# Expert down projection: the 32 leftover middle columns of two steps run together, and GpSimd's order of gathers and scatters changes

## The chip, the cores and the metric

One NeuronCore of a Trainium2 chip runs the whole program in one launch. The metric is the device time of a launch in microseconds. Before the change it is 1369.75 us, the median of three runs (1368.03 to 1370.95).

## What is computed

Six layers are applied in turn to 1024 tokens of 512 values in float32: a small feed-forward layer with a memory, an attention layer, the feed-forward layer again, a mixture of experts, a causal attention layer, and the mixture of experts again with the same weights. The change lies in the mixture of experts, which runs twice:

```python
# x: (1024, 512); 8 experts, the best 2 for each token; F = 800 middle columns
logits = xt @ gate_w.T
top_vals, top_idx = top_k(softmax(logits), 2)       # then normalised to sum 1
h1 = einsum('th,efh->tef', xt, w1)                  # up projections
h3 = einsum('th,efh->tef', xt, w3)
act = silu(h1) * h3                                 # 800 middle columns
expert_out = einsum('tef,ehf->teh', act, w2)        # down projection to 512
y = einsum('te,teh->th', w_full, expert_out)
```

## The kernel before

The 2048 pairs of token and expert are sorted by expert into blocks of 32 rows. Four streams (`NSTR` = 4) of 18 blocks each run side by side, so that an execution of this layer is 18 steps (`NSTEP`), and a step works on four blocks, each with its own expert. Stream j owns rows and columns 32j to 32j+31: TensorE is divided into four column quarters, and stream j's results go to PSUM partitions 32j to 32j+31.

A step p has these parts:

- GpSimd gathers 128 rows of tokens from DRAM into `XB` (L880, two buffers). VectorE turns them by blocks of 32 by 32 (L1119).
- `up(p)` on TensorE (L954): 4 chunks of 128 contraction rows, 2 halves of 400 columns, 2 matrices, 4 streams. Each float32 matmul is two instructions in the trace, so that this is 128 instructions. They use all 128 rows of the array and one column quarter each. It needs the step's weights in two halves (`w13_in[0]`, `w13_in[1]`).
- ScalarE applies silu (L1001), VectorE multiplies (L1125) and turns the 800 columns into `ACT_T` (the first 768, L1141) and `ACT_R` (the last 32, L1138).
- `down(p)` on TensorE: the main part (L972) runs over 6 chunks of 128 middle columns, 48 instructions. Then comes the tail (L975) for the last 32 middle columns: for each stream one matmul with 32 contraction rows, 8 instructions. Stream j's activations and weights (`W2B`) lie in partitions 32j to 32j+31, so that its tail uses row quarter j and column quarter j of the array. Main part and tail add into the same PSUM bank, 4 + p % 2. The tail's last instruction raises `m_y`.
- ScalarE copies the bank to `YB` (L1007, two buffers) and GpSimd scatters it to DRAM (L892).

TensorE's order is up(0), up(1), down(0), up(2), down(1) and so on to up(17), down(16), down(17). Between the last two downs there is no up.

SyncE issues the weight loads, in an order written out by hand. Of a step it does: four value loads from the table of experts (L842), the first half of the up weights of the four streams once TensorE is past the first half of the up before (`m_wf`, L848), the second half once that up is done (`m_h`, L850). Then it waits for `m_y` of the down before (L857) and issues, for each stream, the main down weights (L803; stream 3 in two pieces) and the 32 tail rows (L810), nine DMAs. All are conditional: one whose stream keeps its expert is issued, and moves nothing. Main and tail loads count on one semaphore, `w2_in`, and `down(p)` waits for all nine (L965). A first load is made on a guess of the expert before the routing is known (L829 to L833).

GpSimd's order (L885 to L893) is gather 0, gather 1, and then for each p gather p+2 and scatter p. Scatter p waits for ScalarE's copy of step p (`m_yc`).

Other waits on `m_y`: ScalarE's copy (L1007), and VectorE before it overwrites `ACT_T` and `ACT_R` (L1135).

Of the kernel before, what the change touches and what calls it, by code (L numbers as in the profile page):

```python
# [14 lines left out]
P = 128  # L15
# [33 lines left out]
def macaron_program(nc, A, out, stages=6):  # L49

    ctx = ExitStack()
    with ctx:
# [159 lines left out]
        XBT = take([2, C, P])  # L212
        AC = take([FF])
        ACT_T = take([2, FC, P])
        ACT_R = take([2, SR])
        YB = take([2, D])
        W2B = take([D])
        W2_LAST = take([FC // 2, D])
        W13, W2A = [None] * NSTR, [None] * NSTR
        for j in (2, 0, 1):  # L220
# [565 lines left out]
        yl_in = [sem(f"yl_in{i}") for i in range(NT)]  # L786
        LOADS = NSTEP + 1
        N13 = 16 * NSTR
        N2 = 16 * (2 * NSTR + 1)
        assert NSTEP % 2 == 0  # L790

        def up_in(eng, j, a, e, cond=None):

# [11 lines left out]
                              cond=cond).then_inc(w2_in, 16)  # L805
                at += n

        def tail_in(eng, j, e, cond=None):

            eng.dma_start(W2B[SR * j:SR * j + SR], A["w2b"][e].rearrange("e p d -> p (e d)"),  # L810
                          cond=cond).then_inc(w2_in, 16)

        def guess(j):

            return slice(2 * j, 2 * j + 1)
# [7 lines left out]
        def sp_moe(eng, k, f):  # L823
# [2 lines left out]
                eng.wait_ge(s_h, NT * k + i + 1)  # L826
                eng.dma_start(HD[i * P:(i + 1) * P, :], h[:, i, :]).then_inc(S("s_hd"), 16)
            eng.wait_ge(stage_end, 4 * k)
            for j in range(NSTR):  # L829
                tail_in(eng, j, guess(j))  # L830
            eng.wait_ge(S("s_hd"), 16 * NT * (f + 1))
            eng.wait_ge(S("s_lgt"), 4 * f + 4)
            guess_in(eng, f, last)  # L833
# [3 lines left out]
            for p in range(NSTEP + 1):  # L837
                if p < NSTEP:
                    now = []
                    for j in range(NSTR):  # L840
                        q = j * NSTEP + p
                        x = eng.value_load(EBX[q:q + 1, 0:1], min_val=0, max_val=2 * NE - 1)  # L842
                        now.append((bass.ds(x % NE, 1), x >= NE))
                    for a in range(2):
                        if p == 0:
                            eng.wait_ge(w13_in[a], N13 * (LOADS * f + 1))
                        elif a == 0:
                            eng.wait_ge(S("m_wf"), NSTEP * f + p)  # L848
                        else:
                            eng.wait_ge(S("m_h"), 2 * (NSTEP * f + p))  # L850
                        for j in range(NSTR):
                            up_in(eng, j, a, *now[j])
                if p >= 1:
                    if p == 1:
                        eng.wait_ge(w2_in, N2 * (LOADS * f + 1))
                    else:
                        eng.wait_ge(S("m_y"), NSTEP * f + p - 1)  # L857
                    for j in range(NSTR):
                        down_in(eng, j, *late[j])
                        tail_in(eng, j, *late[j])  # L860
                late = now
            if f == 0:
                sp_attn1_weights(eng)
# [9 lines left out]
        def pool_moe(eng, link, k, f):  # L873
# [11 lines left out]
            gather(0)  # L885
            gather(1)
            eng.wait_ge(S("s_sidx"), f + 1)
            for p in range(NSTEP):
                if p + 2 < NSTEP:
                    gather(p + 2)  # L890
                eng.wait_ge(S("m_yc"), NSTEP * f + p + 1)
                eng.indirect_dma_start(YS[:, :], bass.IndirectOffsetOnAxis(ap=SIDX[:, p:p + 1], axis=0),  # L892
                                       YB[:, p % 2, :], None).then_inc(y_out[p % 2], 16)  # L893
            if f == 0:
                pool_front(eng, link, k + 1)

        def pe_moe(eng, k, f):
# [65 lines left out]
            def down(p):  # L963
                G, u = NSTEP * f + p, p % 2
                eng.wait_ge(w2_in, N2 * (LOADS * f + p + 2))  # L965
                eng.wait_ge(S("m_at"), G + 1)
                if G >= 2:
                    eng.wait_ge(S("m_yc"), G - 1)
                for c in range(FC):
                    for j in range(NSTR):  # L970
                        part = W2A[j][c // W2A[j][0].shape[1]]
                        eng.matmul(PS[SR * j:SR * j + SR, 4 + u, :], ACT_T[:, u, c, SR * j:SR * j + SR],  # L972
                                   part[:, c % part.shape[1], :], start=(c == 0), stop=False, skip_group_check=True)
                for j in range(NSTR):
                    mm = eng.matmul(PS[SR * j:SR * j + SR, 4 + u, :], ACT_R[SR * j:SR * j + SR, u, :],  # L975
                                    W2B[SR * j:SR * j + SR, :], start=False, stop=True, skip_group_check=True)
                mm.then_inc(S("m_y"), 1)

            for p in range(NSTEP):
                up(p)  # L980
# [7 lines left out]
        def act_moe(eng, link, k, f):  # L988
# [5 lines left out]
            for p in range(NSTEP + 1):  # L994
                G = NSTEP * f + p
                if p < NSTEP:
                    for hf in range(2):
# [1 line left out]
                        if G > 0:  # L999
                            eng.wait_ge(S("m_at"), G)  # L1000
                        eng.activation(AC[:, hf * FH:(hf + 1) * FH], PS[:, 2 * hf, 0:FH], ACT.Silu).then_inc(S("m_sg"), 1)  # L1001
                if p >= 1:
                    u = (p - 1) % 2
                    eng.wait_ge(S("m_y"), G)
                    if p >= 3 or f == 1:
                        eng.wait_ge(y_out[u], 16 * (NSTEP // 2 * f + (p - 1) // 2))
                    eng.copy(YB[:, u, :], PS[:, 4 + u, :]).then_inc(S("m_yc"), 1)  # L1007
            for u in range(2):
                eng.wait_ge(y_out[u], 8 * NSTEP * (f + 1))
# [6 lines left out]
        def dve_moe(eng, link, k, f):  # L1016
# [110 lines left out]
            for p in range(NSTEP):  # L1127
# [4 lines left out]
                product(G, 1)  # L1132
                eng.wait_ge(S("m_act"), 2 * G + 2)
                if G >= 2:
                    eng.wait_ge(S("m_y"), G - 1)  # L1135
                for a in range(NSTR):
                    rows = slice(SR * a, SR * a + SR)
                    eng.transpose(ACT_R[rows, u, :], AC[rows, FC * P:FF])  # L1138
                    for b in range(NSTR):
                        src = AC[rows, 0:FC * P].rearrange("p (c f) -> p c f", c=FC)  # L1140
                        tr = eng.transpose(ACT_T[SR * b:SR * b + SR, u, :, rows], src[:, :, SR * b:SR * b + SR])  # L1141
# [549 lines left out]
```

## Time and profile before

| | |
|---|---|
| median of 3 runs | 1369.75 us (1368.03 to 1370.95) |
| profiled execution, its own time | 1372.15 us |
| its span in the trace | 1370.4 us |
| mean granted TensorE clock | 0.937 of full |
| TensorE matmuls busy | 1185.6 us (87%) |
| VectorE busy | 866.3 us (63%) |
| ScalarE busy | 350.0 us (26%) |
| GpSimd busy | 123.5 us (9%) |
| first mixture of experts, first up to last tail | 217.7 to 532.0 us of the span |
| second mixture of experts, the same | 1015.7 to 1347.3 us of the span |

The profile has a chain of waits (the work that ended last, followed back from the last instruction), a timeline of each engine, a list of who waited for whom, and the busy time, granted clock and DMA traffic of any stretch. A granted clock of 1.00 is 2.4 GHz, and 0.50 is 1.2 GHz. TensorE's matmuls are pipelined, so that one record is longer than the distance between two starts; the distances of the starts tell what a group costs. The records of four streams start at almost the same time and count as one group.

### The profile page before, as it was taken

How to read it: one execution, taken by the hardware profiler on the slowest of the kernel's cores; microseconds unless marked ns; L12 is line 12 of the kernel's file. 1: busy time of each engine (PE TensorE's matmuls, PEld its weight loads, DVE VectorE, ACT ScalarE, POOL GpSimd, SP SyncE). 2: the span in 40 equal slices, each digit the busy share in tenths (PEclk: the TensorE clock that was granted, in tenths of full speed). 3: DMA queues.
4: the chain of work that ended last, by engine and by line, in shares of the span. 5: the costliest groups of instructions: out<-in, count | busy, mean ns of one | idle time of the engine just before them, and what ended most of it. 6: DMA issues, size and time to landing. Idle time of an engine off the chain costs nothing.

```text
span 1370.4 us, 26531 instructions
## 1 busy us (share of the span) xinstructions
PE 1185.6 (87%) x9782; PEld 486.0 (35%) x9782; DVE 866.3 (63%) x2491; ACT 350.0 (26%) x723; POOL 123.5 (9%) x151
## 2 busy tenths in 40 slices
PE   6799756999999994688789999999759889999982
PEld 3477422333333331333334444433323323333320
DVE  4731476767787763654888888841358657777753
ACT  4434420000000000121166666674100000000000
POOL 1100010111111100220100000000100111111100
PEclk9899887999999997799999999999869999999995
DMA  9000332047503244239514331005640533514545
GB/s 368 11 1 1 142 137 99 32 175 280 216 33 128 94 155 170 94 101 128 101 42 78 58 56 29 2 2 215 279 167 17 224 123 138 185 65 140 179 179 206
DMA packets 44521, 166.15 MB, mean 121 GB/s; under 512 B 7613, under 2 KB 14355, under 8 KB 40039
## 3 DMA queue, kind: packets, MB, share of 16 engines
q1 hardware_dynamic: 34415, 137.28, 30.3%
q0 software_dynamic: 5760, 18.88, 4.0%
q10 hardware_dynamic: 4216, 8.29, 2.7%
q8 instruction: 77, 1.26, 0.4%
q14 instruction: 53, 0.43, 0.1%
HBM read 786.00 MB, written 22.03 MB: 590 GB/s over the span
## 4 chain that ended last, share of the span: by engine, by line
PE 75%; DVE 12%; DMA 5%; issue 3%; ACT 3%; SPq 1%; POOL 1%; ACTq 0%; POOLq 0%; DVEq 0%
PE PS L954 28%; PE PS L972 13%; PE PS L1397 5%; PE PS L1360 4%; PE PS L1384 4%; DVE PS L1519 3%; PE PS L975 2%; PE PS L706 2%; PE PS L689 2%; PE PS L1424 2%; PE PS L1343 2%; PE PS L479 2%; PE PS L493 1%; DMA HH<-in_w 1%; PE PS L1348 1%
## 5 line engine op out<-in xcount | busy, mean ns | idle before, releaser
L954 PE MATMUL PS<-arena 128*32 128x400 f32 x3456 | 399.0, 504 | 8.0 <-DMA HH<-in_w 4.0
L954 PE MATMUL PS<-HH,arena 128*32 128x400 f32 x1152 | 398.5, 504 | 0.0
L1119 DVE STREAM_TRANSPOSE arena<-arena 32x128 f32<-32x128 f32 x544 | 164.7, 303 | 144.8 <-DMA arena<-h_scratch,RT 137.6
L954 PEld LDWEIGHTS PS<-arena 128*32 128x32 f32 x3456 | 141.4, 111 | 261.7 <-issue 257.2
L1519 DVE CUSTOM_DVE_ANT_0 PS<-PS,U 128x128 f32<-128x128 f32 (+7 forms) x256 | 188.0, 783 | 59.3 <-PE PS L1360 58.5
L1141 DVE STREAM_TRANSPOSE arena<-arena 32x192 f32<-32x192 f32 x576 | 211.4, 367 | 7.2
L972 PE MATMUL PS<-arena 128*32 128x512 f32 x1512 | 197.7, 604 | 15.0 <-DMA arena<-in_w2b 15.0
L1465 ACT ACTIVATE arena<-PS 128x512 f32<-128x512 f32 (+3 forms) x384 | 165.2, 496 | 74.0 <-PE PS L1387 48.4
L1001 ACT ACTIVATE arena<-PS 128x400 f32<-128x400 f32 x72 | 36.3, 504 | 363.4 <-PE PS L954 363.4
L954 PEld LDWEIGHTS PS<-HH,arena 128*32 128x32 f32 x1152 | 124.6, 111 | 0.0
L1360 PE MATMUL PS<-arena 96*128 96x512 bf16 (+3 forms) x384 | 104.0, 332 | 17.6 <-DVE arena L1519 13.7
L1384 PE MATMUL PS<-arena 99*128 99x512 bf16 (+3 forms) x384 | 111.9, 330 | 5.1 <-DVE arena L1503 2.2
L972 PEld LDWEIGHTS PS<-arena 128*32 128x32 f32 x1512 | 55.9, 112 | 142.9 <-issue 125.2
L972 PE MATMUL PS<-HH,arena 128*32 128x512 f32 x216 | 104.2, 621 | 0.0
L892 POOL DMA_INDIRECT y_scratch<-arena,RT x36 | 35.7, 991 | 573.7 <-ACT arena L1007 573.7
L1397 PE MATMUL PS<-arena 128*32 128x512 f32 (+3 forms) x768 | 80.2, 497 | 0.0
L1007 ACT COPY arena<-PS 128x512 f32<-128x512 f32 x36 | 21.1, 586 | 223.9 <-PE PS L975 223.9
L479 PE MATMUL PS<-ident,HH 128*128 128x128 f32 x128 | 29.0, 382 | 53.7 <-DVE HH L454 52.7
L1343 PE MATMUL PS<-HH,arena 128*128 128x512 f32 x128 | 63.6, 622 | 0.8 <-ACTq L158 0.8
L1360 PEld LDWEIGHTS PS<-arena 96*128 96x128 bf16 x384 | 31.3, 99 | 92.1 <-DVE arena L1519 62.8
L1125 DVE TENSOR_TENSOR arena<-arena,PS 128x400 f32<-128x400 f32 x72 | 39.3, 569 | 34.4 <-ACT arena L1001 33.1
L1384 PEld LDWEIGHTS PS<-arena 99*128 99x128 bf16 x384 | 37.1, 98 | 55.5 <-ACT arena L1465 34.1
(246 smaller groups left out, 1156.3 us busy)
## 6 DMA issues: line engine op xcount, KB each, us to landing
arena<-in_w SPq DMA_DIRECT2D x228, 1600.0 KB
arena<-in_w2a SPq DMA_DIRECT2D x114, 1536.0 KB
HH<-in_w SPq DMA_DIRECT2D x76, 1600.0 KB
HH<-in_w2a SPq DMA_DIRECT2D x38, 768.0 KB
arena<-in_w2a SPq DMA_DIRECT2D x38, 768.0 KB
arena<-in_w2b SPq DMA_DIRECT2D x152, 64.0 KB
arena<-split_scratch SPq DMA_DIRECT2D x72, 128.0 KB, 6.5
split_scratch<-arena SPq DMA_DIRECT2D x48, 128.0 KB, 2.3
```

The costliest lines, as they stand in the source:

```text
L479: tr = eng.transpose(PS[:, FB[k][i % 2], c * P:(c + 1) * P], HS[k][0][:, i, c * P:(c + 1) * P], ident[:])
L954: mm = eng.matmul(PS[SR * j:SR * j + SR, 2 * hf + m, 0:FH], XBT[:, u, c, SR * j:SR * j + SR], W13[j][:, c // 2, m, c % 2, hf * FH:(hf + 1) ...
L972: eng.matmul(PS[SR * j:SR * j + SR, 4 + u, :], ACT_T[:, u, c, SR * j:SR * j + SR], part[:, c % part.shape[1], :], start=(c == 0), stop=Fal ...
L1119: tr = eng.transpose(XBT[SR * b:SR * b + SR, u, :, SR * a:SR * a + SR], src[:, :, SR * b:SR * b + SR])
L1125: eng.tensor_tensor(half, half, PS[:, 2 * hf + 1, 0:FH], ALU.mult).then_inc(S("m_act"), 1)
L1141: tr = eng.transpose(ACT_T[SR * b:SR * b + SR, u, :, rows], src[:, :, SR * b:SR * b + SR])
L1343: mm = eng.matmul(PS[:, at + par, :], wcols[:, par], HS[k][1][:, c, J * HT_:(J + 1) * HT_], start=(c == 0), stop=(c == C - 1))
L1360: mm = eng.matmul(PS[:, b + lo // HT_, 0:hi - lo], QT[0:KS, slot, h, i * P:(i + 1) * P], KT[0:KS, slot, h, lo:hi], start=True, stop=True)
L1384: mm = eng.matmul(bank[:, 0:hi - lo], KT[0:KS + 3, slot, h, i * P:(i + 1) * P], QT[0:KS + 3, slot, h, lo:hi], start=True, stop=not diag, s ...
L1397: mm = eng.matmul(PS[32 * h:32 * h + 32, 7, lo - J * HT_:HT_], VA[:, i, (GH * g + h) * VC:(GH * g + h) * VC + 32], PB[:, n % 3, h, 0:hi - lo],
L1465: eng.activation(PB[:, (n // GH) % 3, h, 0:hi - lo], PS[:, 4 + n % 3, 0:hi - lo], ACT.Exp, scale=SCALE1).then_inc(S("s_p"), 1)
L1519: eng.tensor_tensor_reduce(scores, scores, MASKW[:, T - wide:T], 1.0, HOLE, ALU.add, ALU.max, MP[:, g % 2, h, i:i + 1]).then_inc(S("s_md"), 1)
```

## The change

- The tail of the steps 0 to 15 is done in pairs. `down(p)` of an even step ends after its main part. `down(p)` of the odd step behind it does its own main part and then the tails of both. For stream j the even step's tail uses row quarter j and the odd step's tail row quarter (j+1) % 4; both use column quarter j, and they add into different PSUM banks (4 and 5). Steps 16 and 17 keep a tail each.
- The tail weights get two buffers: the old one, and `U`, a tensor that this layer did not use. The tail loads are no longer conditional: all four are made in every step, on semaphores of their own, and the guessed tail loads are gone. `ACT_R` gets four slots instead of two.
- The main part raises a new semaphore, `m_w2`. SyncE's main loads and VectorE's overwriting wait for it instead of `m_y`. SyncE issues the five main loads of a step first and the four tail loads behind them.
- ScalarE copies both results of a pair behind the odd step's tails. GpSimd gathers up to four steps further ahead, and scatters in pairs: gather 2 to 5, scatters 0 and 1, gathers 6 and 7, scatters 2 and 3, and so on.

```diff
-        ACT_R = take([2, SR])
+        ACT_R = take([4, SR])
         YB = take([2, D])
-        W2B = take([D])
+        W2B = [take([D]), U]
...
-        N2 = 16 * (2 * NSTR + 1)
+        N2 = 16 * (NSTR + 1)
+        N2B = 16 * NSTR
+        w2b_in = [sem("w2b_in0"), sem("w2b_in1")]
...
+        def paired(p):
+            return p < NSTEP - 2
+        def y_done(p):
+            return p + 2 if paired(p) and p % 2 == 0 else p + 1
+        def last_rows(p, j):
+            r = (j + p % 2) % NSTR
+            return slice(SR * r, SR * r + SR)
...
-        def tail_in(eng, j, e, cond=None):
-            eng.dma_start(W2B[SR * j:SR * j + SR], A["w2b"][e].rearrange("e p d -> p (e d)"),
-                          cond=cond).then_inc(w2_in, 16)
+        def tail_in(eng, p, j, e):
+            eng.dma_start(W2B[p % 2][last_rows(p, j)], A["w2b"][e].rearrange("e p d -> p (e d)")).then_inc(w2b_in[p % 2], 16)
...
             eng.wait_ge(stage_end, 4 * k)
-            for j in range(NSTR):
-                tail_in(eng, j, guess(j))
...
                 if p >= 1:
-                    if p == 1:
+                    q = p - 1
+                    if q == 0:
                         eng.wait_ge(w2_in, N2 * (LOADS * f + 1))
                     else:
-                        eng.wait_ge(S("m_y"), NSTEP * f + p - 1)
+                        eng.wait_ge(S("m_w2"), NSTEP * f + q)
                     for j in range(NSTR):
                         down_in(eng, j, *late[j])
-                        tail_in(eng, j, *late[j])
+                    if q >= 2:
+                        eng.wait_ge(S("m_y"), NSTEP * f + y_done(q - 2))
+                    for j in range(NSTR):
+                        tail_in(eng, q, j, late[j][0])
...
-            for p in range(NSTEP):
-                if p + 2 < NSTEP:
-                    gather(p + 2)
+            def scatter(p):
                 eng.wait_ge(S("m_yc"), NSTEP * f + p + 1)
                 eng.indirect_dma_start(YS[:, :], bass.IndirectOffsetOnAxis(ap=SIDX[:, p:p + 1], axis=0),
                                        YB[:, p % 2, :], None).then_inc(y_out[p % 2], 16)
+            for p in range(2, NSTEP):
+                gather(p)
+                if p >= 5 and p % 2 == 1:
+                    scatter(p - 5)
+                    scatter(p - 4)
+            for p in range(NSTEP - 4, NSTEP):
+                scatter(p)
...
+                mm.then_inc(S("m_w2"), 1)
+                if paired(p) and p % 2 == 0:
+                    return
+                ends = (p - 1, p) if paired(p) else (p,)
+                for q in ends:
+                    eng.wait_ge(w2b_in[q % 2], N2B * (NSTEP // 2 * f + q // 2 + 1))
                 for j in range(NSTR):
-                    mm = eng.matmul(PS[SR * j:SR * j + SR, 4 + u, :], ACT_R[SR * j:SR * j + SR, u, :],
-                                    W2B[SR * j:SR * j + SR, :], start=False, stop=True, skip_group_check=True)
-                mm.then_inc(S("m_y"), 1)
+                    for q in ends:
+                        rows = last_rows(q, j)
+                        mm = eng.matmul(PS[SR * j:SR * j + SR, 4 + q % 2, :], ACT_R[rows, (NSTEP * f + q) % 4, :],
+                                        W2B[q % 2][rows, :], start=False, stop=True, skip_group_check=True)
+                mm.then_inc(S("m_y"), len(ends))
...
-                if p >= 1:
-                    u = (p - 1) % 2
-                    eng.wait_ge(S("m_y"), G)
-                    if p >= 3 or f == 1:
-                        eng.wait_ge(y_out[u], 16 * (NSTEP // 2 * f + (p - 1) // 2))
+                if p >= 1 and not paired(p - 1):
+                    ready = (p - 1,)
+                elif p >= 2 and p % 2 == 0:
+                    ready = (p - 2, p - 1)
+                else:
+                    ready = ()
+                for q in ready:
+                    u = q % 2
+                    eng.wait_ge(S("m_y"), NSTEP * f + y_done(q))
+                    if q >= 2 or f == 1:
+                        eng.wait_ge(y_out[u], 16 * (NSTEP // 2 * f + q // 2))
                     eng.copy(YB[:, u, :], PS[:, 4 + u, :]).then_inc(S("m_yc"), 1)
...
                 if G >= 2:
-                    eng.wait_ge(S("m_y"), G - 1)
+                    eng.wait_ge(S("m_w2"), G - 1)
                 for a in range(NSTR):
                     rows = slice(SR * a, SR * a + SR)
-                    eng.transpose(ACT_R[rows, u, :], AC[rows, FC * P:FF])
+                    eng.transpose(ACT_R[last_rows(p, a), G % 4, :], AC[rows, FC * P:FF])
```

## Rows read from the trace of the kernel before

**Rows 1.** Chain of waits, two steps: start us, length us, what

```profile
265.41 10.88 PE PS L954 x128
276.29 5.15 PE PS L972 x48
282.43 10.88 PE PS L954 x128
...
1143.33 10.88 PE PS L954 x128
1154.21 5.15 PE PS L972 x48
```

**Rows 2.** Busy time of stretches, one step of either layer; PEclk, DMA share, GB/s last

```profile
265.41:282.43 17.02, 17.02 (x188) 5.76 (x192) 13.27 (x41) 1.59 (x3) 1.96 (x2) 1.00 0.55 188
1143.33:1160.36 17.03, 17.03 (x189) 5.77 (x192) 12.61 (x39) 1.59 (x3) 1.96 (x2) 1.00 0.13 47
```

**Rows 3.** Timeline of TensorE around one tail: start, length, line, form

```profile
263.80 0.61 PE L972 MATMUL PS<-arena 128*32 128x512 f32 x4
264.35 1.06 PE L975 MATMUL PS<-arena 32*32 32x512 f32 x8
265.34 0.54 PE L954 MATMUL PS<-arena 128*32 128x400 f32 x3
265.36 0.52 PE L954 MATMUL PS<-HH,arena 128*32 128x400 f32 x1
```

**Rows 4.** Timeline of TensorE, the five waits for weights in brackets

```profile
523.99 0.88 PE L972 MATMUL PS<-arena 128*32 128x512 f32 x3 [3.21 <-DMA arena<-in_w2b]
...
1083.17 0.54 PE L954 MATMUL PS<-arena 128*32 128x400 f32 x3 [2.40 <-DMA HH<-in_w]
...
1092.08 0.54 PE L954 MATMUL PS<-arena 128*32 128x400 f32 x3 [1.63 <-DMA HH<-in_w]
...
1118.42 1.07 PE L972 MATMUL PS<-arena 128*32 128x512 f32 x3 [3.73 <-DMA arena<-in_w2b]
...
1338.62 1.07 PE L972 MATMUL PS<-arena 128*32 128x512 f32 x3 [8.02 <-DMA arena<-in_w2b]
```

**Rows 5.** Chain of waits around the wait at 1118.42

```profile
1102.81 1.04 PE PS L975 x8
1103.86 0.13 SPq L803
...
1108.20 10.17 DMA arena<-in_w2b
...
1118.42 6.90 PE PS L972 x48
```

**Rows 6.** SyncE's issues before that wait

```profile
1104.10 0.08 SPq L803 DMA_DIRECT2D arena<-in_w2a  x1
1104.45 0.07 SPq L810 DMA_DIRECT2D arena<-in_w2b  x1
1104.81 0.07 SPq L803 DMA_DIRECT2D arena<-in_w2a  x1
1105.16 0.07 SPq L810 DMA_DIRECT2D arena<-in_w2b  x1
1105.51 0.36 SPq L803 DMA_DIRECT2D arena<-in_w2a  x1
1106.15 0.34 SPq L810 DMA_DIRECT2D arena<-in_w2b  x1
```

**Rows 7.** Chain of waits at the first layer's last down

```profile
519.79 1.04 PE PS L975 x8
520.84 0.13 SPq L803
...
523.99 7.05 PE PS L972 x48
```

**Rows 8.** Timeline of VectorE there, the last turn before down(17)

```profile
521.18 1.53 DVE L1141 STREAM_TRANSPOSE arena<-arena 32x192 f32<-32x192 f32 x4
```

**Rows 9.** Stretches in and behind the waits; PEclk, DMA share, GB/s last

```profile
1083.17:1090.44 7.27, 7.27 (x64) 2.93 (x64) 0.00 (x0) 0.00 (x0) 0.81 (x1) 0.77 0.94 386
1092.08:1097.66 5.58, 5.58 (x68) 2.23 (x72) 4.17 (x13) 0.50 (x1) 0.00 (x0) 1.00 0.02 3
1118.42:1125.30 6.88, 6.88 (x52) 1.69 (x56) 6.60 (x21) 0.00 (x0) 0.00 (x0) 0.77 0.01 2
```

**Rows 10.** SyncE's issues between two downs, all but the last pair without traffic

```profile
1064.04 0.08 SPq L803 DMA_DIRECT2D arena<-in_w2a  x1
...
1066.90 0.07 SPq L810 DMA_DIRECT2D arena<-in_w2b  x1
1069.95 1.60 SPq L794 DMA_DIRECT2D arena<-in_w  x3
```

**Rows 11.** Who waited for whom: us in total, times, longest us

```profile
POOL y_scratch L892 <- ACT arena L1007: 573.7, 36, 30.9
DVE arena L1119 <- DMA arena<-h_scratch,RT: 137.6, 28, 8.6
```

More of the change, by code:

```diff
@@ L971, in down @@
                         part = W2A[j][c // W2A[j][0].shape[1]]
-                        eng.matmul(PS[SR * j:SR * j + SR, 4 + u, :], ACT_T[:, u, c, SR * j:SR * j + SR],
-                                   part[:, c % part.shape[1], :], start=(c == 0), stop=False, skip_group_check=True)
-                for j in range(NSTR):
-                    mm = eng.matmul(PS[SR * j:SR * j + SR, 4 + u, :], ACT_R[SR * j:SR * j + SR, u, :],
-                                    W2B[SR * j:SR * j + SR, :], start=False, stop=True, skip_group_check=True)
-                mm.then_inc(S("m_y"), 1)
+                        mm = eng.matmul(PS[SR * j:SR * j + SR, 4 + u, :], ACT_T[:, u, c, SR * j:SR * j + SR],
+                                        part[:, c % part.shape[1], :], start=(c == 0), stop=False, skip_group_check=True)
+                mm.then_inc(S("m_w2"), 1)
[4 more added lines that the diff above has]
+                    eng.wait_ge(w2b_in[q % 2], N2B * (NSTEP // 2 * f + q // 2 + 1))
+                for j in range(NSTR):
+                    for q in ends:
[3 more added lines that the diff above has]
+                mm.then_inc(S("m_y"), len(ends))
             for p in range(NSTEP):
```

## The prediction

> **What bounds the kernel now.** I read the chain of waits first, because the page's totals mix six layers. In both expert layers the chain is TensorE alone, step after step: 10.88 us of up matmuls, 5.15 us of the main part of down, and then the tail [rows 1]. From one up to the next it is 282.43 - 265.41 = 17.02 us. The busy times of such a step say the same: TensorE is busy for all of its 17.02 us at a granted clock of 1.00, VectorE for 12.6 to 13.3 us, ScalarE for 1.6, GpSimd for 2.0 [rows 2]. So what a step costs is what TensorE does in it, and every microsecond taken from it counts as long as nothing else comes late. The exceptions are five places where TensorE waits for weights [rows 4]: one at the first layer's last down (3.21 us), three around one change of experts in the second layer (2.40, 1.63 and 3.73 us), one at its last down (8.02 us).
>
> **The tail, in detail.** The timeline has the last main group at 263.80, the tail at 264.35 and the next up at 265.34 [rows 3]. The main part's twelve groups take 5.15 us, 0.43 us a group [rows 1]. Without a tail the next up would start one group after 263.80, at 264.23. So a tail costs 265.34 - 264.23 = 1.11 us: two waves of four matmuls (0.43 us each, like a main group of equal length) and 0.25 us of changes in and out. The eight records together are only 1.06 us long, while each group of four in the main part is 0.61 us long; so the four streams' tails, each in a row quarter and a column quarter of its own, already run side by side.
>
> **Removed: one tail in two steps.** The steps 0 to 15 of both layers make 16 pairs, and each pair gives back one whole tail, 1.11 us, if the eight matmuls of two steps take as long as the four of one. Do they? No row shows two matmuls that share a column quarter and differ in their row quarter. From below: the other direction is known, for in up and main down four streams share all rows and start 0.02 us apart [rows 3], so the first record of a fourth stream comes about 0.007 us behind the third; with four more streams in each of two waves that is 0.05 us. From above: if two row quarters of one column quarter take turns, a pair needs four waves and 0.86 us more. I take 0.05 us, since the nearest row is that of four streams sharing a resource without taking turns, and each of the eight has weights, cells and a bank of its own. That gives 16 x (1.11 - 0.05) = 17.0 us.
>
> The Trainium skill ("TensorEngine Tiling (Array Packing)", section Restrictions and Gotchas) speaks against it: different row tiles cannot use one PSUM bank at the same time. The four tails of a step are four row tiles in one bank, and their eight records last 1.06 us in all, so by this trace the rule does not hold for tiles in different columns; here two tiles of the same column use two banks. Were it to hold in the pair, the four waves above would be the least of it. The skill's "TensorE: Matmul & The Clock Gate", section Part 3, gives 10.6 times for 16 tiles of 32 by 32; by that page eight would cost an estimated 0.02 us over four, and the sum would be 17.4 instead of 17.0 us. No row here shows it.
>
> **Where that is not gained.** Up(4) of the second layer waits 2.40 us for its first half of weights [rows 4], behind down(2), whose tail goes. The load's start hangs on up(3) and on SyncE's queue, not on the tail, so it lands when it did, and 1.1 us of the gain turns into wait. The second wait (1.63 us) only keeps its end. The sum is 15.9 us.
>
> **Moved: the main loads wait for the main part, not for the tail.** Three of the five waits end with `in_w2b`, the last of nine loads.
> - 1118.42, down(4): the step before is odd and keeps its (double) tail. SyncE starts at 1103.86, when the tail is over [rows 5]; it would start when the main part is, 1.05 us earlier. The first load that moves bytes is the fifth issue, at 1105.51, 1.41 us behind the first, because an issue costs 0.35 us even without traffic [rows 6]; without the two tail loads between it comes 0.70 us sooner. The two moving tail loads, 128 KB or 0.3 us at the 386 GB/s of [rows 9], no longer stand before the end. Together 2.0 us; the wait shrinks to about 1.7 us.
> - 523.99, down(17): nothing moves; the wait is nine issues [rows 7]. By SyncE alone five issues from 519.8 would end near 521.7. But VectorE turns this step's columns until 521.18 + 1.53 = 522.71 [rows 8], so this is what is late next: 523.99 - 522.71 = 1.3 us gained, 1.8 us of wait left.
> - 1338.62, down(17): the load of a changed expert. It starts 1.05 us earlier and a tail load is no longer waited for (0.15 us): 1.2 us.
>
> **The clock.** After the 3.21 and the 3.73 us the main part took 7.05 and 6.90 us instead of 5.15 [rows 5, 7], at a granted clock of 0.77 [rows 9] between the levels of 1.2 and 2.4 GHz; after 2.40 us of waiting the clock was 0.77 as well, after 1.63 us it stayed 1.00 [rows 9]. Waits of 1.7 and 1.8 us are left. They lie between the row that lost the clock and the one that kept it, nearer to the latter. Both kept: 1.9 + 1.75 = 3.65 us; both lost: 0. I take half, 1.8 us.
>
> **Added or moved without a price, and its cover.** The tail loads move 256 KB in every step, 0.6 us of DMA time; a step of 17 us had a DMA share of 0.55 and 0.13 [rows 2]. They are needed five to seventeen us after their issue. An issue with traffic takes 0.34 us and not 0.07 [rows 6], so SyncE's queue grows by 4 x 0.27 = 1.1 us. Behind it stand the value loads and the next up loads: these came at 1069.95, 5.9 us behind the first of the nine at 1064.04 [rows 10], about when `m_wf` allows them. Before an even step SyncE starts 1.05 us sooner, which pays for it; before an odd step it does not, and the up loads start up to 1.1 us later. The cover is the time from there to the next up, some 11 us. GpSimd's scatters wait for ScalarE 573.7 us in all, and VectorE 137.6 us for gathered rows [rows 11]; the latter wait mostly goes, hidden by TensorE in any case. The new wait of the paired copies has the next up's 10.88 us for cover before down needs the bank. Where the profile shows no stall, earlier gathers give nothing.
>
> **Sum.** 15.9 + 2.0 + 1.3 + 1.2 + 1.8 = 22.2 us. The profiled execution took 1372.15 us, so 1349.95; it lies 2.4 us above the median of 1369.75, which makes 1347.5 us. With the clock kept and the pair at no cost it is 1345; with the clock lost and 0.6 us of tail loads in each of four stalls it is 1352.
>
> **The rivals.**
> - *Two row quarters of a column take turns.* For: no row shows the contrary, and both feed the same 32 PSUM partitions. Against: separate banks, and rows shared without turns. 16 x 0.86 = 13.8 us less: 1361 us. Should half of it overlap, 1354.
> - *The extra issues make up loads late.* Before odd steps the load starts 1.1 us later; where a change of experts had less room than that, TensorE waits. For: the second layer already has such a wait. Against: up waited for weights only twice in 36 steps. If eight changes lose 0.7 us each: 1353 us.
> - *Slower: the eight matmuls form a queue.* Each shares its row quarter or its column quarter with the one before it. If sharing either blocks issue, sixteen instructions follow each other, 16 x 0.43 = 6.9 us in place of 0.9, and a pair loses 6.0 - 1.1 = 4.9 us: 16 x 4.9 = 78 us slower, less the 6 us gained at the waits, about 1442 us. It decides from the fifth wave on: above 2.2 us of tails a pair loses. Against: the main part shares rows without blocking.
> - *It doesn't do what it says:* the pair is right but the double buffer or the copies stall TensorE for 1 us or more in each pair, by a wait that I have not seen: 1368 us, no change.
>
> **Chances.** Forecast 0.72, loads late 0.09, take turns 0.12, no change 0.02, queue 0.05. A difference of 0.2% (2.7 us) is about what a measurement can tell here. Faster 0.93, same 0.02, slower 0.05. The forecast's own 1343.5 to 1352 holds some 0.65; with late loads and the turns up to 1361.5 it is 0.83.
>
> **What would show it.** In the timeline of the kernel after, an even step's last main group is followed by up after 0.43 us, and the pair's sixteen tail records are about 1.1 us long in all (1.9: take turns; 7: a queue). Two steps take 32.98 us and not 34.05. The waits for `in_w2b` before down are gone; those for `in_w2a` are about 1.7 and 6.8 us, and the first layer's last down waits for VectorE. The wait before up(4) has grown to 3.5 us. Wrong would be: new waits of up for `in_w` at other steps, tails waiting for `in_w2b`, or ScalarE's copies ending later than the next up.

## The result, and the profile after

The change makes the kernel faster: 1354.91 us (median of five runs, 1353.53 to 1358.38) against 1368.21 us for the kernel before in five runs; ratio 0.9886, interval 0.9860 to 0.9912. That is 13 us, or 1.1%, where 22 us were forecast; it lies inside the stated range of 1343.5 to 1361.5 us, but above the part of it, 1343.5 to 1352 us, that was the forecast's own; the rest belonged to the rivals. The profiled execution took 1354.91 us, its span is 1353.1 us.

How much of the 17.3 us between the two profiled spans belongs to the change? The two expert layers, from their first up matmul to their last tail, are cut out as stretches. First before, then after (length, TensorE busy and its records, and so on; granted clock, DMA share and GB/s last):

```profile
217.65:532.03 314.38, 309.82 (x3312) 105.19 (x3312) 220.96 (x668) 29.41 (x55) 32.40 (x33) 0.99 0.35 123
1015.65:1347.34 331.69, 314.58 (x3312) 106.31 (x3312) 220.89 (x667) 29.40 (x54) 32.43 (x33) 0.97 0.36 131
```

```profile
213.95:523.17 309.22, 302.67 (x3312) 111.53 (x3312) 221.80 (x668) 28.62 (x55) 32.35 (x33) 0.99 0.41 139
1004.25:1329.06 324.81, 308.01 (x3312) 107.93 (x3312) 221.65 (x668) 28.62 (x55) 32.32 (x33) 0.96 0.42 147
```

The layers are 5.2 and 6.9 us shorter, 12.0 us together. The other 5.2 us of the spans lie outside, 3.7 us of them ahead of the first layer, where the first up matmul starts at 217.7 before and at 214.0 after. In the ten traces below that start lies between 212.1 and 217.0, so most of this is a difference between executions, as far as one trace of the kernel before can tell. The layers' 12.0 us and the medians' 13.3 us agree.

**A pair takes what was forecast.** The chain of waits in an undisturbed stretch of the first layer (start, length, what), which answers to [rows 1]:

```profile
446.21 10.75 PE PS L978 x128
456.95 5.15 PE PS L996 x48
462.10 1.02 PE PS L1007 x16
463.12 10.88 PE PS L978 x128
474.00 5.15 PE PS L996 x48
479.15 0.99 PE PS L978 x9
```

Up is now L978, the main part L996, the tails L1007. Two steps take 479.15 - 446.21 = 32.94 us, before 34.05. The even step's up follows the main part at once (474.00 + 5.15 = 479.15). The timeline of the pair's tails answers to [rows 3]:

```profile
461.46 0.64 PE L996 MATMUL PS<-arena 128*32 128x512 f32 x4
462.03 0.61 PE L1007 MATMUL PS<-arena 32*32 32x512 f32 x1
...
462.08 0.61 PE L1007 MATMUL PS<-U,arena 32*32 32x512 f32 x1
462.49 0.59 PE L1007 MATMUL PS<-arena 32*32 32x512 f32 x1
...
463.05 0.54 PE L978 MATMUL PS<-arena 128*32 128x400 f32 x3
```

Eight matmuls start within 0.05 us (462.03 to 462.08), the next eight 0.46 us later. A record with `U` is an odd step's tail; it runs beside the even step's in the same column quarter.

**The new waits.** From the timeline of TensorE only the rows in which it waits in these steps, with the wait in brackets; they answer to [rows 4]:

```profile
277.92 0.54 PE L978 MATMUL PS<-arena 128*32 128x400 f32 x3 [0.52 <-DMA HH<-in_w]
283.88 0.54 PE L978 MATMUL PS<-arena 128*32 128x400 f32 x3 [0.39 <-DMA HH<-in_w]
311.97 0.54 PE L978 MATMUL PS<-arena 128*32 128x400 f32 x3 [0.30 <-DMA HH<-in_w]
346.76 0.54 PE L978 MATMUL PS<-arena 128*32 128x400 f32 x3 [1.64 <-DMA HH<-in_w]
430.10 0.54 PE L978 MATMUL PS<-arena 128*32 128x400 f32 x3 [0.32 <-DMA HH<-in_w]
515.13 1.00 PE L996 MATMUL PS<-arena 128*32 128x512 f32 x3 [2.03 <-issue]
1071.05 0.54 PE L978 MATMUL PS<-arena 128*32 128x400 f32 x3 [2.56 <-DMA HH<-in_w]
1080.67 0.54 PE L978 MATMUL PS<-arena 128*32 128x400 f32 x3 [2.35 <-DMA HH<-in_w]
1108.60 0.63 PE L996 MATMUL PS<-arena 128*32 128x512 f32 x3 [3.60 <-DMA arena<-in_w2a]
1321.28 1.07 PE L996 MATMUL PS<-arena 128*32 128x512 f32 x3 [6.94 <-DMA arena<-in_w2a]
```

The first five are new: in the first layer up did not wait for weights before, and now it does at the steps 4 (both halves), 6, 8 and 13. The chain of waits shows what they cost with the slower restarts behind them; up(2) and up(10) of the first layer:

```profile
244.45 10.75 PE PS L978 x128
...
379.92 10.75 PE PS L978 x128
```

Eight steps in 135.47 us. Four undisturbed pairs would take 4 x 32.94 = 131.76, the kernel before took 8 x 17.02 = 136.2. So over these eight steps 3.7 of the 4.4 us that the pairs earn are given back.

The longest of the new waits shows how it comes about. Before, the last of the up loads that up(8) needs first was issued 8.6 us behind the start of up(7), and 8.5 us before up(8):

```profile
333.44 0.54 PE L954 MATMUL PS<-arena 128*32 128x400 f32 x3
342.00 0.12 SPq L794 DMA_DIRECT2D HH<-in_w  x1
350.46 0.54 PE L954 MATMUL PS<-arena 128*32 128x400 f32 x3
```

After, it is issued 10.5 us behind the start of up(7), and up(8) could begin at 346.76 - 1.64 = 345.12, only 5.6 us later:

```profile
329.02 0.54 PE L978 MATMUL PS<-arena 128*32 128x400 f32 x3
339.49 0.12 SPq L810 DMA_DIRECT2D HH<-in_w  x1
```

The load takes 7.1 us to land, as the chain of waits says:

```profile
339.49 7.14 DMA HH<-in_w
```

Of the 2.8 us that are missing, SyncE's later issue takes 1.9 and the shorter way to up(8) 0.9.

### The profile page after: what moved, and what is told of

The parts are those of the page before. It is cut to its first block, busy times and chain, and to the rows that moved or that the text cites. A ratio compares the mean times of both kernels' runs of the same rounds, so it can differ in the third digit from the quotient of the medians.

```text
span 1353.1 us, 26539 instructions
## 1 busy us (share of the span) xinstructions
PE 1165.3 (86%) x9782; PEld 491.5 (36%) x9782; DVE 868.1 (64%) x2491; ACT 348.4 (26%) x723; POOL 123.4 (9%) x151
## 4 chain that ended last, share of the span: by engine, by line
PE 69%; DVE 11%; DMA 8%; issue 4%; ACT 3%; SPq 3%; POOL 1%; ACTq 0%; POOLq 0%; DVEq 0%
PE PS L978 25%; PE PS L996 12%; PE PS L1435 5%; PE PS L1398 5%; PE PS L1422 4%; DMA HH<-in_w 4%; PE PS L706 3%; DVE PS L1557 2%; PE PS L689 2%; PE PS L1462 2%; PE PS L1381 2%; DMA arena<-y_scratch 1%; PE PS L479 1%; PE PS L493 1%; PE PS L1007 1%
## 5 line engine op out<-in xcount | busy, mean ns | idle before, releaser
L978 PE MATMUL PS<-arena 128*32 128x400 f32 x3456 | 402.7, 508 | 12.0 <-DMA HH<-in_w 8.1
L978 PE MATMUL PS<-HH,arena 128*32 128x400 f32 x1152 | 402.1, 508 | 0.0
L978 PEld LDWEIGHTS PS<-arena 128*32 128x32 f32 x3456 | 148.7, 111 | 260.6 <-issue 254.1
L996 PE MATMUL PS<-arena 128*32 128x512 f32 x1512 | 197.1, 603 | 12.6 <-DMA arena<-in_w2a 10.5
L978 PEld LDWEIGHTS PS<-HH,arena 128*32 128x32 f32 x1152 | 126.2, 111 | 0.0
L1398 PE MATMUL PS<-arena 96*128 96x512 bf16 (+3 forms) x384 | 104.0, 332 | 17.6 <-DVE arena L1557 13.7
L996 PEld LDWEIGHTS PS<-arena 128*32 128x32 f32 x1512 | 58.2, 112 | 137.4 <-issue 125.0
L996 PE MATMUL PS<-HH,arena 128*32 128x512 f32 x216 | 103.5, 617 | 0.0
L897 POOL DMA_INDIRECT arena<-h_scratch,RT x36 | 35.2, 978 | 364.0 <-DVE arena L1157 315.0
```

The lines of the kernel that those rows point to most:

```text
L978: mm = eng.matmul(PS[SR * j:SR * j + SR, 2 * hf + m, 0:FH], XBT[:, u, c, SR * j:SR * j + SR], W13[j][:, c // 2, m, c % 2, hf * FH:(hf + 1) ...
L996: mm = eng.matmul(PS[SR * j:SR * j + SR, 4 + u, :], ACT_T[:, u, c, SR * j:SR * j + SR], part[:, c % part.shape[1], :], start=(c == 0), sto ...
L1398: mm = eng.matmul(PS[:, b + lo // HT_, 0:hi - lo], QT[0:KS, slot, h, i * P:(i + 1) * P], KT[0:KS, slot, h, lo:hi], start=True, stop=True)
```

## The experiments

All ratios are to the kernel before, run on the same chip in the same rounds. "Steps 2 to 10" is the time from the start of up(2) to that of up(10), which holds the change's new waits; the undisturbed value is 131.8 us with pairs and 136.2 us without.

| kernel | ratio (interval) | layer 1, steps 2 to 10 | layer 2, steps 2 to 10 | wait before layer 2's down(4) |
|---|---|---|---|---|
| before | 1 | 136.2 | 147.7 | 3.73 |
| the change | 0.9886 (0.9860 to 0.9912) | 135.5 | 146.0 | 3.60 |
| the change again | 0.9877 (0.9842 to 0.9912) | 134.8 | 146.0 | 3.56 |
| tail loads of steps 2 to 17 left out | 0.9755 (0.9720 to 0.9790) | 133.0 | not comparable | |
| conditional tail loads | 0.9841 (0.9811 to 0.9871) | 133.9 | 144.2 | 2.93 |
| same row quarter | 0.9916 (0.9882 to 0.9950) | 136.8 | 146.0 | 2.48 |
| late gathers | 0.9907 (0.9873 to 0.9941) | 134.9 | 145.0 | 3.24 |
| split only, no pairs | 0.9957 (0.9936 to 0.9977) | 136.2 | 147.1 | 2.39 |
| late tail issue | 0.9886 (0.9845 to 0.9928) | 135.2 | 142.2 | 2.61 |
| conditional and late | 0.9834 (0.9803 to 0.9866) | 132.4 | 142.7 | 2.96 |
| the same again | 0.9838 (0.9809 to 0.9868) | 132.7 | 142.8 | 2.92 |
| the same, scatters apart | 0.9851 (0.9817 to 0.9885) | 133.2 | 142.6 | 1.88 |

My theory after the comparison: the pairs run side by side as forecast, and the unconditional tail loads, together with the shorter steps, make up's weights late. The rivals: the shorter steps alone do it, or GpSimd's earlier gathers.

### Tail loads left out

```diff
-                    if q >= 2:
-                        eng.wait_ge(S("m_y"), NSTEP * f + y_done(q - 2))
-                    for j in range(NSTR):
-                        tail_in(eng, q, j, late[j][0])
+                    if q < 2:
+                        for j in range(NSTR):
+                            tail_in(eng, q, j, late[j][0])
...
-                    eng.wait_ge(w2b_in[q % 2], N2B * (NSTEP // 2 * f + q // 2 + 1))
+                    eng.wait_ge(w2b_in[q % 2], N2B * (f + 1))
```

> The change, with the tail loads of the steps 2 to 17 left out (the tails of those steps use old weights, so that the output is another; 128 of the 144 loads of 64 KB are gone). Theory (the extra loads, by their issues on SyncE and their bytes, make up's weights late): the waits of up for in_w in the first layer, about 4 us at steps 4 to 13, are gone, and the first layer takes 305 us instead of 309.2; ratio to before 0.983 to 0.985. Rival (the shorter steps alone ask for the weights sooner than the DMA can bring them): the waits stay within 1 us of the change's, ratio 0.988.

The first layer took 303.8 us instead of 309.2; of its five waits one of 0.65 us is left. Steps 2 to 10 took 133.0 us: 2.5 of the 3.7 us are the loads' (1.8 of 3.0 us by the second trace of the change), 1.2 us stay with the shorter steps and whatever else the change moved. So the theory holds for the larger part; that the rest is its rival's is not shown. The old tail weights change the tokens and with them the second layer's routing; TensorE did not wait at step 4 there, and the layer took 309.0 us. The ratio of 0.9755 contains that and tells nothing of the loads.

### Conditional tail loads

```diff
-                        now.append((bass.ds(x % NE, 1), x >= NE))
+                        now.append((bass.ds(x % NE, 1), x >= NE, x))
...
-                        tail_in(eng, q, j, late[j][0])
-                late = now
+                        either = None if q < 2 else (late[j][2] // NE + older[j][2] // NE) >= 1
+                        tail_in(eng, q, j, late[j][0], either)
+                late, older = now, late
```

> The change, with the tail loads made conditional again from step 2 on: a stream's tail rows are loaded where its expert changed in this step or in the one before (the two steps use two buffers). All 144 are still issued, some 15 to 25 in a layer move bytes. Theory (issues held up behind other traffic, and bytes): most of the gain of the run without tail loads, ratio 0.984 to 0.986. Rival (the number of issues, not what they move): like the change, 0.988.

0.9841, as the theory said; its interval overlaps the change's, but steps 2 to 10 took 133.9 us against 135.5 and 134.8 in the first layer and 144.2 us against twice 146.0 in the second. The queue rows of the two pages show the traffic (queue, packets, MB, share of the 16 engines), first with the change, then with the conditional loads:

```profile
q1 hardware_dynamic: 40319, 145.35, 32.9%
```

```profile
q1 hardware_dynamic: 35375, 138.60, 31.3%
```

6.75 MB and 4944 packets less. The number of issues is the same, so it is what they move that costs. This does not yet tell the bytes from SyncE's queue: an issue that moves nothing also takes SyncE less time, 0.07 us in the median instead of 0.33.

### Same row quarter

```diff
-            r = (j + p % 2) % NSTR
+            r = j
```

> The change, with the odd step's tail in the same row quarter as the even step's, so that both matmuls of a stream use one 32 by 32 tile of the array and must follow each other. Theory (the pair is side by side because the row quarters differ): a pair's sixteen records are about 1.95 us long instead of 1.1, an odd step 0.86 us longer, the whole 16 x 0.86 = 13.8 us slower than the change, so about as fast as before, ratio 0.998. Rival (row quarters of one column take turns anyway and the gain is only the missing change in and out): same time as the change, 0.988.

The timeline of a pair's tails:

```profile
257.53 1.07 PE L996 MATMUL PS<-arena 128*32 128x512 f32 x8
258.53 1.08 PE L1007 MATMUL PS<-arena 32*32 32x512 f32 x8
259.41 1.06 PE L1007 MATMUL PS<-U,arena 32*32 32x512 f32 x8
260.40 0.54 PE L978 MATMUL PS<-arena 128*32 128x400 f32 x3
```

Now the odd step's eight start 0.88 us behind the even step's, and the next up 260.40 - 258.53 = 1.87 us behind the first tail instead of 1.02. That is the pair's four waves, and it shows that the other row quarter is what puts the two side by side. But the kernel lost less than the 13.6 us that its tails grew by: 0.9916, not 0.998. The first layer grew by 1.8 us (311.0 against 309.2), not by 6.8. Of the roughly 5 us in between, 2.5 are smaller losses at the waits: those of up were 1.1 us, not 3.2. The other 2.6 are luck with the clock: up(0) took 12.16 us instead of 13.05, and the main part of the last down 5.36 us instead of 7.05. In the second layer the waits before up(4) were 2.13 and 4.02 us, longer in sum than the change's 2.56 and 2.35, and the one before down(4) 2.48 us instead of 3.60. So longer tails fill, in part, time in which TensorE would wait for weights.

### Late gathers

```diff
-                if p >= 5 and p % 2 == 1:
-                    scatter(p - 5)
-                    scatter(p - 4)
-            for p in range(NSTEP - 4, NSTEP):
+                if p >= 3 and p % 2 == 1:
+                    scatter(p - 3)
+                    scatter(p - 2)
+            for p in range(NSTEP - 2, NSTEP):
```

> The change, with GpSimd's gathers two steps later: gathers 2 and 3, scatters 0 and 1, gathers 4 and 5, scatters 2 and 3. Theory (gathering ahead is hidden by TensorE either way): within 0.2% of the change, 0.988. Rival (early gathers move traffic into the busy stretch of the weight loads and make up late): waits of up for in_w shrink by over 1 us and the ratio is 0.986 or less. Other rival (the gathers ahead are needed): VectorE waits for rows again, TensorE waits for VectorE, ratio above 0.990.

0.9907, its interval holds the change's 0.9886. The waits of up were 0.16, 1.40, 0.42 and 0.29 us at the steps 4, 6, 8 and 10, 2.3 us in all. But only the first of them is for weights. The second and third are for VectorE:

```profile
305.44 5.05 DVE L1157 STREAM_TRANSPOSE arena<-arena 32x128 f32<-32x128 f32 x16 [9.31 <-DMA arena<-h_scratch,RT]
311.68 0.54 PE L978 MATMUL PS<-arena 128*32 128x400 f32 x3 [1.40 <-DVE arena L1163]
345.26 0.54 PE L978 MATMUL PS<-arena 128*32 128x400 f32 x3 [0.42 <-DVE arena L1163]
```

The gather for the next step stands behind the two scatters of the pair, VectorE gets its rows late (it waited for rows 98.3 us in all, against 9.0 with the change), and its product, whose PSUM banks up(6) needs, comes late in turn. So the second rival is there: the change needs its early gathers, by up to 1.8 us in the first layer, since the copies and scatters of a pair come together. What the experiment was to settle it leaves open. The waits of up for weights in the first layer are nearly gone, but where TensorE waits for VectorE a wait for weights would be hidden; steps 2 to 10 took 134.9 us against 135.5 and 134.8. In the second layer the two waits of up(4) for weights were 5.9 us, with the change 4.9. Early gathers as a part of the cause of the new waits are neither shown nor excluded.

### The split alone

```diff
-        N2 = 16 * (2 * NSTR + 1)
+        N2 = 16 * (NSTR + 1)
+        w2b_in = sem('w2b_in')
...
-                        eng.wait_ge(S("m_y"), NSTEP * f + p - 1)
+                        eng.wait_ge(S("m_w2"), NSTEP * f + p - 1)
                     for j in range(NSTR):
                         down_in(eng, j, *late[j])
+                    if p == 1:
+                        eng.wait_ge(w2b_in, 16 * NSTR * (LOADS * f + 1))
+                    else:
+                        eng.wait_ge(S("m_y"), NSTEP * f + p - 1)
+                    for j in range(NSTR):
                         tail_in(eng, j, *late[j])
...
+                mm.then_inc(S("m_w2"), 1)
+                eng.wait_ge(w2b_in, 16 * NSTR * (LOADS * f + p + 2))
```

> The kernel before, with the main part's semaphore alone: m_w2 raised by the main part, SyncE's five main loads wait for it and go first, the four conditional tail loads behind the tail, on a semaphore of their own. No pairs. Theory (what this part gives is what the trace of the change showed at the last downs: 1.2 us and 1.1 us; and, without a second scatter and unconditional tail loads in the way, up to 2 us before the second layer's down(4)): 2 to 5 us faster than before, ratio 0.9965 to 0.9985. Rival (the part gives nothing by itself, the pairs give all): 1.000.

0.9957: loads that wait for the main part are worth 6 us by the ratio, a little more than the 2 to 5 expected. Part of what its trace gains is the clock: the first layer is 2.9 us shorter, 1.7 of them since the main part of its last down took 5.36 us instead of 7.05. The wait before the second layer's down(4) in its timeline:

```profile
1112.82 0.63 PE L978 MATMUL PS<-arena 128*32 128x512 f32 x3 [2.39 <-DMA arena<-in_w2a]
```

It fell from 3.73 to 2.39 us, by 1.34 where I had 2.0; in the change itself it fell by 0.13 only. Steps 2 to 10 of the second layer gained just 0.6 us: the second wait before up(4) was 3.33 us instead of 1.63, and the half up behind it took 8.33 us instead of 5.58. The first layer's last down waited 2.03 us, as in the change.

### Late tail issue

```diff
                         for j in range(NSTR):
                             up_in(eng, j, a, *now[j])
+                        if a == 0 and held:
+                            tails(*held)
+                            held = None
```

> The change, with SyncE's four tail loads of steps 0 to 15 issued later: behind the next first-half up loads instead of before the value loads. Their number and bytes stay. Theory A (what makes up's weights late is that SyncE is held 1.8 to 3.7 us at these issues): up's waits in the first layer fall from 3.2 us to under 1 us, ratio 0.985. Theory B (it is the bytes and packets, 0.7 us of all DMA engines a step): waits stay near 3 us or move to the tails, ratio 0.988.

This was to tell the held queue from the moved bytes. With the change SyncE's queue is held indeed; its issues between up(7) and up(8) of the first layer, which answer to [rows 10]:

```profile
328.36 1.11 SPq L819 DMA_DIRECT2D arena<-in_w2a  x3
329.75 0.07 SPq L819 DMA_DIRECT2D HH<-in_w2a  x1
330.10 0.07 SPq L819 DMA_DIRECT2D arena<-in_w2a  x1
330.60 3.71 SPq L826 DMA_DIRECT2D arena<-in_w2b  x4
337.59 1.53 SPq L810 DMA_DIRECT2D arena<-in_w  x3
```

Four tail loads hold it for 3.71 us (4.61 us when the change was run again), and the up loads come 9.2 us behind the first main load; at the same step before it was 6.2 us (333.80 to 340.03). But taking them out of the way gained nothing by itself: 0.9886. In the first layer the waits moved, in part to the tails:

```profile
326.98 0.58 PE L1017 MATMUL PS<-arena 32*32 32x512 f32 x1 [0.46 <-DMA U<-in_w2b]
344.91 0.54 PE L988 MATMUL PS<-arena 128*32 128x400 f32 x3 [0.80 <-DMA HH<-in_w]
428.43 0.58 PE L1017 MATMUL PS<-arena 32*32 32x512 f32 x1 [1.52 <-DMA U<-in_w2b]
```

So theory B: the waits of up were 2.2 us and those of the tails 2.0. Step 8 shows both halves of the cost. The last load for up(8) was issued 8.0 us behind the start of up(7), as without tail loads, so the queue was free again. But it took 8.8 us to land where the kernel without tail loads had it in at most 8.1, and up(8) waited 0.80 us. In that stretch the DMA engines are nearly full (busy share 0.97 from 328 to 347 us), and here what moves beside the up load makes it later. In the second layer the late issue gained 3.8 us over steps 2 to 10, which the ratio does not show within its interval.

### Conditional and late

Both edits together, `tails()` with the condition of the second experiment.

> The change, with conditional tail loads (as in the second run) and their later issue. Both theories: no wait of up in the first layer but what the up loads make themselves, under 1 us; the first layer about 305 us; ratio 0.982 to 0.984. If it is the same as the conditional loads alone (0.984), the place of the issues does not matter once they move nothing.

0.9834, and 0.9838 when run again. The chain has up(2) and up(10) of the first layer at

```profile
242.77 10.75 PE PS L989 x128
...
375.18 10.75 PE PS L989 x128
```

132.4 us, 0.6 us above the undisturbed pairs. This is the fastest kernel with the whole computation: 1347.13 us against 1352.95 for the change in the same rounds. Each of its six runs (1346.29 to 1349.34) was faster than each of the change's six (1349.64 to 1357.62). The intervals of the two ratios overlap; the traces of either, twice, do not: 132.4 and 132.7 us against 135.5 and 134.8 in the first layer, 142.7 and 142.8 against 146.0 and 146.0 in the second.

### The change again

> The change itself, on the chip and in the rounds of these runs, for comparison: 0.9886 as before, within 0.986 to 0.991. The waits of up in the first layer (steps 4, 6, 8 and 13, 3.2 us) come again within 1 us if they belong to the kernel and not to one execution.

0.9877. The waits of up in the first layer were 0.23, 0.56 and 0.54 us at the steps 4, 6 and 8, and the main part of a down waited 0.84 us at step 6: 2.2 us, not 3.2. They belong to the kernel, but their places shift by a step and their sizes by a microsecond.

### Scatters apart

```diff
             for p in range(2, NSTEP):
+                if p >= 6:
+                    scatter(p - 6)
                 gather(p)
-                if p >= 5 and p % 2 == 1:
-                    scatter(p - 5)
-                    scatter(p - 4)
-            for p in range(NSTEP - 4, NSTEP):
+            for p in range(NSTEP - 6, NSTEP):
                 scatter(p)
```

> The change with conditional and late tail loads, and with GpSimd's two scatters of a pair no longer behind each other: one gather stands between them, so that the second one's 256 KB come some 4 us later. Theory (the second scatter delays the main down loads issued at the same time): the wait before the second layer's down(4) falls from 2.96 us to 2.4 us, what it is with the split alone; all in all within 0.1% of the run without it. Rival (the scatters don't matter there): 2.9 us or more.

> The conditional and late tail loads again, for comparison on the same chip: ratio to before 0.983 within 0.981 to 0.986, and waits of up in the first layer under 1 us.

The wait before down(4) fell to 1.88 us, further than expected: as far as one trace against two can show, the second scatter of a pair does delay the main loads issued with it. The two waits before up(4) grew at the same time, from 2.17 and 1.90 to 3.10 and 3.39 us, and the whole stayed the same (142.6 and 142.8 us). It looks as if a transfer moved out of one load's way stood in another's; no further run tests it.

## Why the prediction was right, and by how much it missed

The direction and the mechanism of the gain held; the sum was 22.2 us and the layers gave 12.0. The result of 1354.91 us lies above the forecast's own 1343.5 to 1352, near the 1353 of the rival "loads late" and the 1354 that half an overlap of the tails would have given. The range held it because it took in the rivals; the traces say that it was the late loads, and that the tails overlap in full. Term by term, from the two traces:

| term | forecast | measured |
|---|---|---|
| 16 tails removed | 17.0 | 17.6 (16 x 1.10) |
| lost at up(4), layer 2 | -1.1 | -0.9 |
| earlier main loads at down(4), layer 2 | 2.0 | 0.1 |
| last down, layer 1 | 1.3 | 1.2 |
| last down, layer 2 | 1.2 | 1.1 |
| clock behind the waits | 1.8 | -0.9 |
| up's new waits in layer 1 | 0, as a rival 5.6 | -4.1 |
| clock in up(0) of both layers | not in the sum | -2.0 |

The measured terms add up to 12.1 us. The one of up(0) (12.29 and 12.65 us before, 13.05 and 13.84 after, granted clock 0.90 and 0.88 up to up(1) before, 0.85 and 0.81 after) changes from trace to trace: 12.1 to 13.9 us in all twelve.

- *The unknown that mattered most was sized well.* No row showed two row quarters of one column quarter at once. I took 0.05 us for them, the timeline after shows 0.05, and with the row quarter the same the four waves of the rival appear. The Trainium skill's rule against different row tiles in one PSUM bank ("TensorEngine Tiling (Array Packing)", Restrictions and Gotchas) was rightly weighed against the trace: in the pair, too, four row quarters write one bank side by side, each to partitions of its own.
- *The step that failed* is "added or moved without a price, and its cover". I set the up loads' delay against some 11 us of cover and called it free. But the cover was not free time: at step 8 of the first layer, where TensorE waits longest, the last load was issued 8.5 us before its use, and in the trace after the change it takes 7.1 us to land. So some 1.3 us were to spare, and 2.8 were taken. No row that I had told how long before up the loads landed. The rival "loads late" had the right mechanism; that its chance was 0.09 was the mistake. Its place was wrong too: I expected it before odd steps, where SyncE starts no sooner, but four of five waits stand before even steps, where the removed tail has shortened the time. The 1.0 us that SyncE starts sooner there did not pay for it: at step 8 its up loads still came 1.9 us later. I had also costed the tail loads by SyncE's unhindered issues, 0.34 us each, where they took up to 3.71 us for four.
- *Up(4) of the second layer* lost what was forecast, in another place. The first wait was to grow to 3.5 us and grew to 2.56; the second was to stay and grew from 1.63 to 2.35. The loads of the second half end the stretch: they let it start 28.21 us behind up(3) (1080.67 - 1052.46), before 28.33 us, so that 0.9 of the 1.0 us of the removed tail is lost.
- *Down(4) of the second layer*: the load did start earlier, its last main piece 2.3 us behind the main part of down(3) where it had been 4.6, but it landed only 0.1 us earlier. The term assumed that nothing else would move. A pair's second scatter and the four unconditional tail loads now do so beside it. Without pairs the term is 1.34 us; without the tail loads' traffic 0.7 us of it come back (3.60 to 2.93), and with the scatters apart another 1.0.
- *The end of the first layer* went as worked out: SyncE is done, and the wait ends with VectorE's last turn. The timeline of VectorE:

```profile
513.54 1.48 DVE L1179 STREAM_TRANSPOSE arena<-arena 32x192 f32<-32x192 f32 x4
```

513.54 + 1.48 = 515.02, and the main part starts at 515.13.
- *The clock* was a fair coin and fell badly: both waits that I had counted at half lost it; they had come out at 3.60 and 2.03 us instead of 1.7 and 1.8. Rows of after, which answer to [rows 9]:

```profile
515.13:522.20 7.07, 7.07 (x52) 2.27 (x56) 0.00 (x0) 0.00 (x0) 0.00 (x0) 0.76 0.25 76
1080.67:1087.77 7.10, 7.10 (x65) 2.52 (x69) 0.56 (x1) 0.51 (x1) 0.00 (x0) 0.76 0.02 5
1108.60:1115.40 6.80, 6.80 (x48) 1.93 (x52) 6.53 (x21) 0.00 (x0) 0.00 (x0) 0.75 0.01 2
```

The second line is a loss that I had not listed: behind the longer second wait before up(4) the half up took 7.28 us by the chain of waits instead of 5.58 [rows 9], 1.7 us. On the other side the second layer's last down took 0.9 us less after its wait than before.

## What to carry to other kernels

When TensorE gets faster, the question is which transfers end just in time today: look for how long before its use each weight lands, not only for waits, since a load with one microsecond to spare is no wait in the profile and becomes one. A load made unconditional to save bookkeeping is not free where transfers already fill the DMA engines; keeping the condition was worth 1 to 2 us a layer over steps 2 to 10 here, and 2 to 3 us together with a later issue. And two float32 matmuls with 32 rows and 32 columns ran in two row quarters of the same columns, on two PSUM banks, in almost the time of one, so it can pay to gather such remainders over steps.

## What the runs showed of the hardware

- Eight 32 by 32 float32 matmuls, two in each column quarter, start within 0.05 us and take the time of four. Two that share one tile follow each other at 0.44 us a wave.
- Whether a wait costs the clock is not settled by its length. The same wait of 2.03 us before the first layer's last down was followed by 5.4 us of main part in six executions and by 7.0 to 7.05 us in five (granted clock 0.76 in the latter).
- A tail load that SyncE issues and that moves 64 KB took it 0.33 us in the median and up to 1.38 us (1.84 us when the change was run again, between up(7) and up(8) of the first layer); whatever stands behind it on SyncE waits.
- Settled by no run: how the 1.2 us that are left without tail loads divide between the shorter steps, the scatters in pairs and the earlier gathers.
